# Two gated cross-attention layers with routed experts: four row scatters moved between two subtractions on GpSimd, value and key copies moved to ScalarE, and the row maxima cut in two parts instead of three

## The chip, the core and the metric

The program runs on one core of a Trainium2 chip. It is one launch, and the metric is its time on the device in microseconds (us). The core has five engines with a queue each, which run side by side and meet only at semaphores: PE (TensorE, the matmuls), DVE (VectorE), ACT (ScalarE), POOL (GpSimd) and SP, which here only issues transfers. Each queue is worked off in the order in which it was written.

## The reference

For x of 16 sequences x 256 tokens x 256 numbers, four updates follow one another:

```python
x = x + tanh(g_xattn[0]) * xattn0(layernorm(x), ctx)   # 16 heads of 16, causal mask, biases bv and bo
x = x + tanh(g_ffn[0])   * ffn0(layernorm(x))          # shared expert + top 2 of 8 experts, silu, hidden 256
x = x + tanh(g_xattn[1]) * xattn1(layernorm(x), ctx)   # 16 heads of 16, keys cut at valid_len = 69, no bias
x = x + tanh(g_ffn[1])   * ffn1(layernorm(x))          # top 2 of 8 experts by cosine score, gelu, hidden 1024
```

In `xattn0` the value is `ctx @ Wv.T + bv`, the probabilities of a row sum to one, and the output is `out @ Wo.T + bo`. In `ffn1` the router projects x, divides by the norm of the projection and multiplies with normalised expert vectors.

## The kernel before

Four phases follow one another: the attention phase of layer 0 (`layer_phase`, with the routing of its tokens to experts in it), the expert phase of layer 0 (`expert_phase`), and the same two for layer 1.

**The steps.** An attention phase is a software pipeline over the 16 sequences, in the line `pipeline(engine, step, B, FIRST, LAST, HEAD, TAIL)` of each engine. Step i works on several sequences at once: i.at(3) is turned and split, i.at(2) is projected to q and k, i.at(1) has its scores computed for their row maxima (`score_head`, `row_maxima`), i.at(0) has them computed again, transposed and with the maximum subtracted (`score_head_t`, `exponentials`, `mix_group`), i.at(-1) is projected with Wo and normalised for the router, and i.at(-2) is routed. Steps -3 to 3 are written out, 4 to 9 are a hardware loop over pairs of steps, 10 to 17 are written out again. Within a step every engine goes through the 16 heads, h = 0 to 15, and at a fixed head it does one other job. The order of the work is thus written out by hand, by the `if h == ...` lines of the four `step` functions.

**q and k.** They are split in three bf16 parts. ACT copies q out of PSUM (`evac_q`), DVE copies k (`evac_k`; in layer 1 it multiplies by a mask of valid keys as well). ACT rounds both (`cut_hi`, L1128), POOL subtracts (L693, the first subtraction), ACT rounds the rest (`cut_mid`, L1132, after head 5), POOL subtracts again (L699, the second subtraction). SP then stacks the parts with 24 or 26 transfers.

**Row maxima.** DVE reduces each head's scores (L839 in layer 1), and after heads 7 and 15 `split_max` cuts the negated maxima of 8 heads in three bf16 parts with four small instructions. PE transposes the parts, ACT copies them and issues three small transfers into three rows of the q stack (`stack_max`, L1139 and L1142).

**Value and output.** PE projects v at head 6, DVE copies it into the padded tile, adding bv in layer 0 (`evac_v`, L823 and L825). PE projects the heads with Wo at head 4.

**The router.** PE computes scores for sequence i.at(-2) at head 1 (`gate_rows_of`, L1360) and ACT copies them. In layer 1 ACT also sums the squares of the projection, DVE floors the sum (`floor_ss`, head 2), POOL takes the power -1/2 (`invert_norm`, L669), and DVE scales the scores (`scale_scores`, L888, head 3) before it picks the two best. This chain runs from PE over ACT, DVE and POOL back to DVE. At head 13 PE transposes the normalised rows of i.at(-1) (`turn_route`), ACT copies them at head 14 (`evac_route`, L1199), and the next step's first projection needs their PSUM bank free.

**The scatters.** `send_rows` sends the 2 x 2 tiles of 128 routed rows of i.at(-2) to their experts' regions in DRAM, with four indirect transfers from POOL (L685). They stand last in POOL's step.

Of the kernel before, what the change touches and what calls it, by code (L numbers as in the profile page):

```python
# [5 lines left out]
P = 128  # L6
# [5 lines left out]
ALU = mybir.AluOpType  # L12
# [36 lines left out]
def pipeline(eng, step, count, first, last, head, tail, while_below=None):  # L49
# [8 lines left out]
    with eng.Fori(lo // 2, hi // 2) as pair:  # L58
        with eng.If(pair * 2 < while_below) if while_below is not None else nullcontext():
            step(Step(pair, 0, count))  # L60
            step(Step(pair, 1, count))
# [156 lines left out]
def layer_phase(nc, keep, routed, layer, x_in, ctx_in, lens, weights, biases, F, up_b, gate, shared, load_experts, xs, x_acc):  # L218
# [10 lines left out]
    HH = H // 2  # L229
    VW = 2 * HD  # L230
# [17 lines left out]
    with ExitStack() as ctx:  # L248
# [43 lines left out]
        max_rest = sb("max_rest", [P, TC, H])  # L292
        max_parts = sb("max_parts", [P, TC, 2, 3, HH], BF16)
        max_t = [pair(f"max_t{half}_", [3 * HH, S], BF16) for half in range(2)]
# [6 lines left out]
        if causal:  # L301
            mask_st = sb("mask_st", [P, 2, P], BF16)
            mask_ts = sb("mask_ts", [P, 2, P], BF16)
            bv_rows = sb("bv_rows", [P, TC, D])
# [98 lines left out]
        wo_spread = sem("wo_spread")  # L403
        x_loaded = sems("x_loaded")
# [28 lines left out]
        max_r1 = sem("max_r1")  # L433
        max_mid = sem("max_mid")
# [61 lines left out]
        N_CONSTS = 3 if causal else 1  # L496
# [4 lines left out]

        FIRST, LAST, HEAD, TAIL = -3, B + 1, 7, 8
# [15 lines left out]
        def _(sp):  # L518
# [5 lines left out]
            if causal:  # L524
                bv, bo = biases
                for c in range(TC):
                    sp.dma_start(bv_rows[:, c], bv.rearrange("(a d) -> a d", a=1).to_broadcast((P, D))).then_inc(consts_loaded, 16)
# [16 lines left out]
            sp.wait_ge(consts_ready, N_READY)  # L544

# [42 lines left out]
        def _(pool):  # L588
# [125 lines left out]
        def _(dve):  # L714
# [43 lines left out]
            ln_stats(0, 0, 0)  # L758
            dve.wait_ge(stats_done, 1)
            ln_mean(0)  # L760
            ln_apply(0, 0)

            dve.wait_ge(r_consts_ready, 1)
            dve.wait_ge(r_loaded, 16 * N_LOADS)
# [1137 lines left out]
```

## Time and profile before

| | us |
|---|---|
| median of 3 runs | 1856.92 |
| lowest, highest of the runs | 1847.23, 1857.61 |
| the profiled execution's own time | 1850.12 |
| its span, first to last instruction | 1848.4 |
| attention phase of layer 0 | about 0 to 567 |
| expert phase of layer 0 | about 567 to 830 |
| attention phase of layer 1 | about 830 to 1380 |
| expert phase of layer 1 | about 1380 to 1848 |

Over the whole span PE is busy 82%, DVE 63%, POOL 39% and ACT 38%, at a mean granted TensorE clock of 0.936. These are averages over four phases that have different limits, so they are to be read by stage. "Idle before" in a row is the time for which an engine stood still ahead of an instruction, and behind it stands the engine that ended the wait.

### The profile page before, as it was taken

How to read it: one execution, taken by the hardware profiler on the slowest of the kernel's cores; microseconds unless marked ns; L12 is line 12 of the kernel's file. 1: busy time of each engine (PE TensorE's matmuls, PEld its weight loads, DVE VectorE, ACT ScalarE, POOL GpSimd, SP SyncE). 2: the span in 40 equal slices, each digit the busy share in tenths (PEclk: the TensorE clock that was granted, in tenths of full speed). 3: DMA queues.
4: the chain of work that ended last, by engine and by line, in shares of the span. 5: the costliest groups of instructions: out<-in, count | busy, mean ns of one | idle time of the engine just before them, and what ended most of it. 6: DMA issues, size and time to landing. Idle time of an engine off the chain costs nothing. (4 is left out here: it accounts for less than half of the span.)

```text
span 1848.4 us, 44757 instructions
## 1 busy us (share of the span) xinstructions
PE 1509.7 (82%) x14491; PEld 1253.5 (68%) x14492; DVE 1165.4 (63%) x3254; ACT 707.4 (38%) x1516; POOL 724.4 (39%) x616
## 2 busy tenths in 40 slices
PE   3799988999982777844888888888752999999997
PEld 2677877788761566633566666666432999999996
DVE  4678876878762334334778888887752455555543
ACT  2344534444430111102354544554421444444443
POOL 4234333344233655553123333333235344446422
PEclk9899999999996999975799999999985999999998
DMA  2433333232214666651323332332225233333322
GB/s 89 106 83 102 95 86 97 81 105 79 80 36 137 115 120 112 115 104 54 99 78 109 92 111 81 110 83 82 71 69 177 59 69 91 91 89 85 87 46 40
DMA packets 211174, 167.03 MB, mean 90 GB/s; under 512 B 23042, under 2 KB 203620, under 8 KB 210788
## 3 DMA queue, kind: packets, MB, share of 16 engines
q1 hardware_dynamic: 179556, 124.56, 24.4%
q0 software_dynamic: 28416, 40.03, 11.7%
q8 instruction: 71, 1.16, 0.3%
q10 hardware_dynamic: 3072, 0.79, 0.2%
q14 instruction: 59, 0.48, 0.1%
HBM read 63.40 MB, written 50.51 MB: 62 GB/s over the span
## 5 line engine op out<-in xcount | busy, mean ns | idle before, releaser
L839 DVE TENSOR_REDUCE a_row_max<-a_scores 128x2 f32<-128x512 f32 x256 | 172.3, 683 | 53.3 <-PE a_scores L1455 49.7
L1693 POOL DMA_INDIRECT out_rows<-e_y,e_token x68 | 110.5, 1625 | 239.2 <-DVE e_y L1749 219.3
L1163 ACT ACTIVATE a_probs<-a_scores_t 128x384 f32<-128x384 f32 (+1 forms) x256 | 132.2, 546 | 163.6 <-PE a_scores_t L1470 82.1
L1163 ACT ACTIVATE a_w_rows<-a_scores_t 128x384 f32<-128x384 f32 (+1 forms) x256 | 138.7, 543 | 142.6 <-PE a_scores_t L1473 74.2
L1775 ACT ACTIVATE e_h<-e_h,t_up_bias 128x256 f32<-128x256 f32 x272 | 110.3, 444 | 206.2 <-PE e_h L1811 206.2
L685 POOL DMA_INDIRECT routed_rows_dram<-r_rows,r_slot x128 | 125.6, 981 | 96.4 <-issue 96.4
L1826 PE MATMUL e_y_bank<-e_down_hi,e_hidden_hi 128*128 128x256 f32 x544 | 157.9, 290 | 0.4 <-DVE e_hidden_lo L1722 0.3
L1811 PE MATMUL e_h<-e_xs_hi,e_up_hi 128*128 128x256 f32 x544 | 155.4, 286 | 1.8 <-DVE e_xs_lo L1714 1.6
L1811 PE MATMUL e_h<-e_xs_lo,e_up_hi 128*128 128x256 f32 x544 | 154.7, 284 | 0.0
L1811 PE MATMUL e_h<-e_xs_hi,e_up_lo 128*128 128x256 f32 x544 | 154.6, 284 | 0.0
L1826 PE MATMUL e_y_bank<-e_down_lo,e_hidden_hi 128*128 128x256 f32 x544 | 153.8, 283 | 0.0
L1826 PE MATMUL e_y_bank<-e_down_hi,e_hidden_lo 128*128 128x256 f32 x544 | 153.8, 283 | 0.0
L1693 POOL DMA_INDIRECT x_mid_dram<-e_y,e_token x76 | 118.5, 1560 | 87.4 <-DVE e_y L1749 45.2
L1744 DVE TENSOR_TENSOR e_y_biased<-e_y_bank,t_down_bias 128x512 f32<-128x512 f32 x72 | 49.8, 691 | 131.2 <-PE e_y_bank L1826 131.2
L798 DVE RECIPROCAL a_den_recip<-a_pv 128x128 f32<-128x128 f32 x128 | 116.9, 936 | 23.3 <-PE a_pv L1494 16.5
L693 POOL TENSOR_TENSOR a_rest<-a_qk,a_parts 128x1024 f32<-128x1024 f32 x32 | 67.9, 2123 | 155.7 <-ACT a_parts L1128 155.7
L1789 PE MATMUL e_turned<-ident,e_xs_rows 128*128 128x128 f32 x296 | 46.9, 282 | 98.6 <-DMA e_xs_rows<-routed_rows_dram 98.4
L1455 PE MATMUL a_scores<-a_k_stack,a_q_stack 98*128 98x256 bf16 x512 | 102.2, 283 | 25.1 <-DVE a_row_max L839 16.5
L1722 DVE TENSOR_TENSOR e_hidden_lo<-e_h,e_hidden_hi 128x512 fp32r<-128x512 f32 x136 | 91.3, 687 | 49.5 <-ACT e_hidden_hi L1764 49.2
L836 DVE TENSOR_REDUCE a_row_max<-a_scores 128x1 f32<-128x128 f32 x256 | 72.6, 284 | 76.1 <-PE a_scores L1452 75.5
L699 POOL TENSOR_TENSOR a_parts<-a_rest,a_parts 128x1024 bf16<-128x1024 f32 x32 | 68.5, 2142 | 116.4 <-ACT a_parts L1132 116.4
L1789 PEld LDWEIGHTS e_turned<-ident,e_xs_rows 128*128 128x128 f32 x296 | 34.1, 143 | 111.3 <-DMA e_xs_rows<-routed_rows_dram 109.9
(267 smaller groups left out, 4673.5 us busy)
## 6 DMA issues: line engine op xcount, KB each, us to landing
a_q_stack<-a_parts SPq DMA_DIRECT2D x384, 64.0 KB, 2.7
a_k_stack<-a_parts SPq DMA_DIRECT2D x384, 64.0 KB, 2.6
e_xs_rows<-routed_rows_dram SPq DMA_DIRECT2D x76, 258.0 KB, 3.2
a_ctx_rows<-in_ctx SPq DMA_DIRECT2D x32, 256.0 KB, 3.1
t_up<-in_L_ffn_W SPq DMA_DIRECT2D x8, 1024.0 KB, 5.0
t_down<-in_L_ffn_W SPq DMA_DIRECT2D x8, 1024.0 KB, 7.6
x_rows<-in_x SPq DMA_DIRECT2D x16, 256.0 KB, 3.1
x_mid_dram<-x_rows SPq DMA_DIRECT2D x16, 256.0 KB, 2.9
```

Of the source, the lines that this page charges most:

```text
L685: pool.indirect_dma_start(out=xs, out_offset=bass.IndirectOffsetOnAxis(ap=slot[p][:, k, c:c + 1], axis=0), in_=rows[p][:, k, c, :], in_off ...
L798: nc.vector.reciprocal(den_recip[:, m, cols], pv[m][:, S + part * P:S + part * P + P]).then_inc(recip_done, 1)
L836: nc.vector.reduce_max(row_max[:, 0, h:h + 1], bank[:, 0:P], AX_X)
L839: nc.vector.reduce_max(row_max[:, :, h], bank[:].rearrange("p (c t) -> p c t", c=TC), AX_X).then_inc(maxed, 1)
L1163: nc.scalar.activation(probs[h % NP][:, 0:width], scores_t[h % 2][:, 0:width], ACT.Exp).then_inc(probs_ready, 1)
L1455: last = nc.tensor.matmul(bank[:, c * S:(c + 1) * S], q[at, h, c * P:(c + 1) * P], k[at, h, :], start=True, stop=True)
L1693: pool.indirect_dma_start(out=x_acc, out_offset=bass.IndirectOffsetOnAxis(ap=token[p][:, c:c + 1], axis=0), in_=y[p][:, c, :], in_offset=N ...
L1722: nc.vector.tensor_tensor(lo, h_bank[g][:], hi.bitcast(F32), ALU.subtract).then_inc(hidden_cut, 1)
L1775: nc.scalar.activation(out, h_bank[g][:, at:at + TS], act_func, bias=routed.up_bias[:, bass.ds(e * FC + fc, 1)]).then_inc(hidden_ready, 1)
L1789: last = nc.tensor.transpose(turned[:, kc * TS + c * P:kc * TS + c * P + P], xs_rows[n][:, c, kc * P:(kc + 1) * P], keep.ident[:])
L1811: last = nc.tensor.matmul(h_bank[g][:, at:at + TS], w[:, kc, fc * P:(fc + 1) * P], x[:, kc, :], start=(kc == 0 and term == 0), stop=(kc == ...
L1826: last = nc.tensor.matmul(y_bank[:, c * D:(c + 1) * D], x[:, fc, c * P:(c + 1) * P], w[:, fc, :], start=(fc == 0 and term == 0), stop=(fc ...
```

## The change

It has six parts, in both attention phases unless a layer is named.

1. `send_rows` works on sequence i.at(-3) instead of i.at(-2), a step later, and stands between POOL's two subtractions, ahead of `invert_norm`. The waits on its rows stand ahead of the first subtraction. POOL's pipeline has one step more at the end.
2. `evac_v` is on ACT, after the exponential behind the head of the v projection. In layer 0 `evac_k` is on ACT too, before the first exponential of the step; in layer 1 it stays on DVE.
3. The bias bv no longer goes into v. Once at the start of layer 0, PE multiplies it with Wo, and DVE adds the product to bo.
4. The negated row maxima have two bf16 parts (`MP = 2`) with two DVE instructions for 8 heads, and `stack_max` issues one transfer instead of three.
5. `copy_rows` on ACT works on i.at(-2) at head 10, instead of i.at(-1) at head 13.
6. In layer 1 the router's scores move from head 1 to 2, the Wo projection from 4 to 5, the v projection from 6 to 8, the ranking from 9 to 10 and the transpose of the context (`turn_ctx`) from 12 to 13, each with what follows it on the other engines. In layer 0 these places are as before, but for `mark_chosen`, which goes from head 6 to 5. On DVE `split_max(i, 1)` stands ahead of `add_shared`.

```diff
+        GATE_AT, O_AT, V_AT, RANK_AT, CTX_AT = (1, 4, 6, 9, 12) if soft else (2, 5, 8, 10, 13)
@@ POOL
+            def rows_are_whole(i):
+                pool.wait_ge(rows_ready, i.at(-3) + 1)
+                pool.wait_ge(rows_copied, i.at(-3) + 1)
             def send_rows(i):
-                b, p = i.at(-2), i.par(-2)
-                wait_apart(pool, rows_ready, b + 1, consts_ready, 1)
-                pool.wait_ge(rows_copied, b + 1)
+                b, p = i.at(-3), i.par(-3)
+                if not i.has(2):
+                    rows_are_whole(i)
                 for k in range(2):
                     for c in range(TC):
                         pool.indirect_dma_start(...)
             def step(i):
                 if i.has(2):
+                    if i.has(-3):
+                        rows_are_whole(i)
                     pool.wait_ge(part_hi, b + 1)
                     nc.gpsimd.tensor_tensor(rest[:], qk[:], parts[p][:, :, 0, :], ALU.subtract).then_inc(part_rest, 1)
+                if i.has(-3):
+                    send_rows(i)
                 if not soft and i.has(-2):
                     invert_norm(i)
...
-                if i.has(-2):
-                    send_rows(i)
-            pipeline(pool, step, B, FIRST, LAST, HEAD, TAIL)
+            pipeline(pool, step, B, FIRST, LAST + 1, HEAD, TAIL + 1)
@@ DVE
-                nc.vector.scalar_tensor_tensor(out=max_rest[:, :, hs], ...).then_inc(max_r1, 1)
-                dve.wait_ge(max_r1, n)
-                nc.vector.tensor_copy(max_parts[:, :, half, 1, :], max_rest[:, :, hs]).then_inc(max_mid, 1)
-                dve.wait_ge(max_mid, n)
-                nc.vector.tensor_tensor(max_parts[:, :, half, 2, :], max_rest[:, :, hs], max_parts[:, :, half, 1, :],
-                                        ALU.subtract).then_inc(max_ready, 1)
+                nc.vector.scalar_tensor_tensor(out=max_parts[:, :, half, 1, :], in0=row_max[:, :, hs], scalar=-1.0,
+                                               in1=max_parts[:, :, half, 0, :], op0=ALU.mult, op1=ALU.subtract).then_inc(max_ready, 1)
+            if causal:
+                dve.wait_ge(bv_mixed, 1)
+                nc.vector.tensor_tensor(bo_rows[:], bo_rows[:], stage[1][:, D:2 * D], ALU.add).then_inc(bo_summed, 1)
...
-                if i.has(2):
+                if not causal and i.has(2):
                     evac_k(i)
@@ ACT
-                for j in range(3):
-                    act.dma_start(q_stack[p][MAX_ROW + j:MAX_ROW + j + 1, half * HH:half * HH + HH, :],
-                                  turned[j * HH:(j + 1) * HH, :]).then_inc(max_stacked[half][p], 16)
+                act.dma_start(q_stack[p][MAX_ROW:MAX_ROW + MP, half * HH:half * HH + HH, :], turned[:]).then_inc(max_stacked[half][p], 16)
+                if causal and i.has(2):
+                    evac_k(i)
                 for h in range(H):
                     if i.has(0):
                         exponentials(i, h)
+                    if h == V_AT + 1 and i.has(1):
+                        evac_v(i)
...
-                    if h == 12 and i.has(3):
+                    if h == CTX_AT and i.has(3):
                         evac_ctx(i)
                     if h == 13 and i.has(1):
                         stack_max(i, 1, 0)
-                    if h == 13 and i.has(-1):
+                    if h == 10 and i.has(-2):
                         copy_rows(i)
```

The queue of POOL in the loop of layer 1, before (one step; a_rest is the first subtraction, r_proj_rnorm is `invert_norm`, a_parts the second subtraction, the DMA row the four scatters):

```order
L693 TENSOR_TENSOR a_rest<-a_qk,a_parts 128x1024
L669 TENSOR_TENSOR r_proj_rnorm<-r_proj_ss_min,a_minus_half 128x2
L699 TENSOR_TENSOR a_parts<-a_rest,a_parts 128x4x256
L661 REGISTER_ALU
L662 TENSOR_TENSOR r_var_eps<-r_mean_var,a_eps 128x2
L664 TENSOR_TENSOR r_rstd<-r_var_eps,a_minus_half 128x2
L618 REGISTER_ALU
L619 TENSOR_TENSOR a_var_eps<-a_mean_var,a_eps 128x2
L621 TENSOR_TENSOR a_rstd<-a_var_eps,a_minus_half 128x2
L685 DMA routed_rows_dram<-r_rows,r_slot 35584x258 x4
```

and the same step of the change:

```order
L706 TENSOR_TENSOR a_rest<-a_qk,a_parts 128x1024
L696 DMA routed_rows_dram<-r_rows,r_slot 35584x258 x4
L676 TENSOR_TENSOR r_proj_rnorm<-r_proj_ss_min,a_minus_half 128x2
L714 TENSOR_TENSOR a_parts<-a_rest,a_parts 128x4x256
L668 REGISTER_ALU
L669 TENSOR_TENSOR r_var_eps<-r_mean_var,a_eps 128x2
L671 TENSOR_TENSOR r_rstd<-r_var_eps,a_minus_half 128x2
L625 REGISTER_ALU
L626 TENSOR_TENSOR a_var_eps<-a_mean_var,a_eps 128x2
L628 TENSOR_TENSOR a_rstd<-a_var_eps,a_minus_half 128x2
```

The four scatters have gone from behind the last small operation to a place directly behind the first subtraction and directly ahead of r_proj_rnorm.

The queue of PE near the end of a step of layer 1, heads 12 to 15, before (a_ctx_rows is `turn_ctx`, a_max_parts the transpose of the maxima, r_rows is `turn_route`, the two a_pv rows a `mix_group`):

```order
L1293 MATMUL a_stage<-ident,a_ctx_rows 128x128 x4
L1321 MATMUL a_stage<-ident,a_max_parts 24x128 x2
L1455 MATMUL a_scores<-a_k_stack,a_q_stack 128x256 x2
L1473 MATMUL a_scores_t<-a_q_stack,a_k_stack 128x256 x2
L1494 MATMUL a_pv<-a_probs,a_v_pad 32x256 x8
L1494 MATMUL a_pv<-a_probs,a_ones_pad 32x256 x8
L1293 MATMUL a_stage<-ident,r_rows 128x128 x4
L1455 MATMUL a_scores<-a_k_stack,a_q_stack 128x256 x2
```

and of the change:

```order
L1349 MATMUL a_stage<-ident,a_max_parts 16x128 x2
L1483 MATMUL a_scores<-a_k_stack,a_q_stack 128x256 x2
L1501 MATMUL a_scores_t<-a_q_stack,a_k_stack 128x256 x2
L1522 MATMUL a_pv<-a_probs,a_v_pad 32x256 x8
L1522 MATMUL a_pv<-a_probs,a_ones_pad 32x256 x8
L1321 MATMUL a_stage<-ident,a_ctx_rows 128x128 x4
L1321 MATMUL a_stage<-ident,r_rows 128x128 x4
L1483 MATMUL a_scores<-a_k_stack,a_q_stack 128x256 x2
```

`turn_ctx` now stands directly ahead of `turn_route`, which waits for ACT's copy of the maxima; on ACT that copy stands behind the copy of what `turn_ctx` writes, as before.

## Rows read from the trace of the kernel before

**Rows 1.** The page, part 5 (costliest groups): busy us, mean ns | idle before
```profile
L839 DVE TENSOR_REDUCE a_row_max<-a_scores 128x2 f32<-128x512 f32 x256 | 172.3, 683 | 53.3 <-PE a_scores L1455 49.7
```

**Rows 2.** Busy time by stage: us, then each engine's busy time (instructions), clock, DMA
```profile
96.00:560.00 464.00, 426.11 (x5508) 356.39 (x5508) 363.65 (x1253) 206.18 (x455) 176.77 (x167) 0.98 0.31 85
...
905.00:1375.00 470.00, 398.32 (x4042) 275.30 (x4035) 380.76 (x1054) 227.95 (x488) 151.45 (x159) 0.99 0.32 89
...
1425.00:1848.40 423.40, 409.02 (x3397) 407.67 (x3396) 215.96 (x387) 192.34 (x409) 174.99 (x82) 0.98 0.34 72
```

**Rows 3.** Timeline of POOL, layer 1: start us, us, instruction [idle before <-releaser]
```profile
1075.16 2.12 POOL L693 TENSOR_TENSOR a_rest<-a_qk,a_parts 128x1024 f32<-128x1024 f32 x1 [4.84 <-ACT a_parts L1128]
1077.39 0.71 POOL L669 TENSOR_TENSOR r_proj_rnorm<-r_proj_ss_min,a_minus_half 128x2 f32<-128x2 f32 x1
1081.94 2.14 POOL L699 TENSOR_TENSOR a_parts<-a_rest,a_parts 128x1024 bf16<-128x1024 f32 x1 [3.83 <-ACT a_parts L1132]
...
1095.34 1.04 POOL L685 DMA_INDIRECT routed_rows_dram<-r_rows,r_slot  x1 [1.33 <-issue]
...
1099.22 0.96 POOL L685 DMA_INDIRECT routed_rows_dram<-r_rows,r_slot  x1 [0.30 <-issue]
1105.10 2.12 POOL L693 TENSOR_TENSOR a_rest<-a_qk,a_parts 128x1024 f32<-128x1024 f32 x1 [4.92 <-ACT a_parts L1128]
```

**Rows 4.** Timeline of DVE, the same step of layer 1
```profile
1076.20 0.69 DVE L839 TENSOR_REDUCE a_row_max<-a_scores 128x2 f32<-128x512 f32 x1 [1.23 <-PE a_scores L1455]
...
1078.22 0.48 DVE L888 TENSOR_SCALAR r_gate_scores<-r_raw_scores,r_proj_rnorm,r_temp_recip 128x8 f32<-128x8 f32 x2 [0.32 <-POOL r_proj_rnorm L669]
...
1082.51 0.69 DVE L839 TENSOR_REDUCE a_row_max<-a_scores 128x2 f32<-128x512 f32 x1 [0.99 <-PE a_scores L1455]
...
1085.50 0.68 DVE L825 COPY a_v_pad<-a_stage 128x512 f32<-128x512 f32 x1
...
1087.03 0.18 DVE L850 SCALAR_TENSOR_TENSOR a_max_rest<-a_row_max,a_max_parts 128x16 f32<-128x16 f32 x1
...
1100.21 1.77 DVE L798 RECIPROCAL a_den_recip<-a_pv 128x128 f32<-128x128 f32 x2 [0.69 <-PE a_pv L1494]
...
1103.19 0.69 DVE L791 TENSOR_TENSOR a_qk<-a_stage,a_valid 128x512 f32<-128x512 f32 x1
```

**Rows 5.** Timeline of PE, the same step of layer 1
```profile
1091.76 1.07 PE L1494 MATMUL a_pv<-a_probs,a_v_pad 128*32 128x256 f32 x16
...
1093.63 0.66 PE L1293 MATMUL a_stage<-ident,r_rows 128*128 128x128 f32 x4
...
1096.61 0.47 PE L1303 MATMUL a_stage<-a_xn_t,a_w_hi 128*128 128x256 f32 x2 [1.45 <-ACT r_xn_t L1199]
...
1104.02 2.02 PE L1360 MATMUL a_stage<-r_gate_w,r_xn_t 128*128 128x264 f32 x8 [1.26 <-DVE a_qk L791]
```

**Rows 6.** Timeline of ACT, the same step of layer 1
```profile
1090.71 0.59 ACT L1155 ACTIVATE a_ctx_t<-a_stage 128x512 fp32r<-128x512 f32 x1
...
1092.36 0.36 ACT L1139 ACTIVATE a_max_t<-a_stage 24x256 bf16<-24x256 bf16 x1
1092.75 1.97 ACTq L1142 DMA_DIRECT2D a_q_stack<-a_max_t  x3
```

**Rows 7.** Timeline of POOL, layer 0, two steps' first subtractions
```profile
186.08 2.12 POOL L693 TENSOR_TENSOR a_rest<-a_qk,a_parts 128x1024 f32<-128x1024 f32 x1 [1.98 <-ACT a_parts L1128]
...
215.94 2.12 POOL L693 TENSOR_TENSOR a_rest<-a_qk,a_parts 128x1024 f32<-128x1024 f32 x1 [1.65 <-ACT a_parts L1128]
```

**Rows 8.** Timeline of PE, layer 0: start, one steady step, the loop's entry
```profile
28.13 1.08 PE L1293 MATMUL a_stage<-ident,a_xn 128*128 128x128 f32 x4 [6.03 <-DVE r_sh_down_bias L767]
...
201.83 0.23 PE L1448 MATMUL a_scores<-a_mask_st,ident 128*128 128x128 bf16 x1 [0.70 <-DVE a_row_max L837]
...
211.16 0.28 PE L1321 MATMUL a_stage<-ident,a_max_parts 128*24 128x128 bf16 x2 [0.76 <-DVE a_max_parts L855]
...
248.92 0.23 PE L1448 MATMUL a_scores<-a_mask_st,ident 128*128 128x128 bf16 x1 [3.81 <-DVE a_row_max L837]
```

More of the change, by code:

```diff
@@ L57, in pipeline @@
     assert lo % 2 == 0 and (hi - lo) % 2 == 0
[L58 to L61, printed above, removed]
+    if lo < hi:
+        with eng.Fori(lo // 2, hi // 2) as pair:
+            with eng.If(pair * 2 < while_below) if while_below is not None else nullcontext():
+                step(Step(pair, 0, count))
+                step(Step(pair, 1, count))
     for i in range(hi, last + 1):
@@ L291, in layer_phase @@
         row_max = sb("row_max", [P, TC, H])
-        max_rest = sb("max_rest", [P, TC, H])
-        max_parts = sb("max_parts", [P, TC, 2, 3, HH], BF16)
-        max_t = [pair(f"max_t{half}_", [3 * HH, S], BF16) for half in range(2)]
+        max_parts = sb("max_parts", [P, TC, 2, MP, HH], BF16)
+        max_t = [pair(f"max_t{half}_", [MP * HH, S], BF16) for half in range(2)]
         probs = [sb(f"probs{n}", [P, 512]) for n in range(NP - 4)] + [w_rows[:, n].rearrange("p c d -> p (c d)") for n in range(4)]
@@ L723, in _ @@
             if causal:
-                nc.vector.tensor_scalar(bo_rows[:], bo_rows[:], keep.tanh_gates[:, gate_col:gate_col + 1], None, ALU.mult).then_inc(bo_gated, 1)
+                for m in range(KC):
+                    src = ctx_rows[1][:, 0, m * P:(m + 1) * P].rearrange("p (half n d) -> p half n d", half=2, d=HD)
+                    for half in range(2):
+                        last = nc.vector.tensor_copy(bv_rows[:, m, :, half, :], src[:, half])
+                last.then_inc(bv_spread, 1)
             else:
@@ L777, in evac_k @@
                 need(dve, part_rest, b)
-                if causal:
-                    dve.wait_ge(k_done, b + 1)
-                    nc.vector.tensor_copy(qk[:, KC:2 * KC, :].rearrange("p c s -> p (c s)"), stage[0][:]).then_inc(k_ready, 1)
-                else:
+                if not causal:
                     n = bass.ds(b, 1)
@@ L992, in step @@
                         row_maxima(i, h)
-                    if h == 2 and not soft and i.has(-2):
+                    if h == GATE_AT + 1 and not soft and i.has(-2):
                         floor_ss(i)
-                    if h == 3 and i.has(-2):
+                    if h == GATE_AT + 2 and i.has(-2):
                         if not soft:
@@ L1222, in step @@
                         cut_mid(i)
-                    if h == 6 and i.has(-2):
+                    if h == GATE_AT + 5 and i.has(-2):
                         route_exps(i)
@@ L1257, in _ @@
             pe.wait_ge(consts_ready, N_READY)
+            if causal:
+                pe.wait_ge(bv_spread, 1)
+                for m in range(KC):
+                    last = nc.tensor.transpose(stage[0][:, m * P:(m + 1) * P], bv_rows[:, m].rearrange("p n half d -> p (n half d)"), keep.ident[:])
+                last.then_inc(bv_turned, 1)
+                pe.wait_ge(bv_copied, 1)
             pe.wait_ge(r_loaded, 16 * N_LOADS)
@@ L1267, in _ @@
                 pe.wait_ge(prep_copied, 3)
+                for m in range(KC):
+                    last = nc.tensor.matmul(stage[1][:, D:2 * D], bv_cols[:, m, :], wo_t[:, m, :], start=(m == 0), stop=(m == KC - 1))
+                last.then_inc(bv_mixed, 1)
+                pe.wait_ge(bo_gated, 1)
             else:
@@ L1514, in step @@
                             mix_group(i, 0, h // GH - 1)
-                    if h == 1 and i.has(-2):
+                    if h == GATE_AT and i.has(-2):
                         gate_rows_of(i)
```

93 lines of the change are left out of this document (50 added, 43 removed).

## The prediction, made before the change was run

> **What bounds the kernel now.** The busy times by stage come first [rows 2]. From 96 to 560 us, the steady part of layer 0's attention phase, PE is busy 426 of 464 us (92%) and DVE 364: PE is nearly the bound. From 905 to 1375 us, layer 1's attention phase, PE is busy 398 of 470 us (85%) and DVE 381 (81%): neither is full, so the step is set by how the two wait for each other. From 1425 us on PE is busy 409 of 423 us in layer 1's experts; the change does not touch that stage, nor layer 0's experts. Then the timelines of one steady step. First subtractions are 29.94 us apart in layer 1 [rows 3] and 29.86 us in layer 0 [rows 7]. In the step of layer 1 DVE's larger waits are 1.23, 0.32, 0.99 and 0.69 us [rows 4], so some 26.7 of its 29.9 us are filled, small gaps counted as filled. PE's larger ones are 1.45 us for ACT's copy of the router's columns and 1.26 us for DVE's copy of k [rows 5]. The reader should see that layer 1 has hardly three us of slack per step on DVE, and that every wait put into DVE's queue there comes out of it.
>
> **1. The scatters behind the first subtraction, layer 1.** This is the largest term. Before, the power -1/2 starts 0.11 us after the first subtraction ends (1077.28 to 1077.39), and DVE waits only 0.32 us for it before it scales the scores [rows 3, 4]. After, four scatters stand between the two. Four take 4.84 us from the start of the first to the end of the last (1095.34 to 1100.18) [rows 3]; with 0.17 us ahead of the first, about 5.0 us. The chain counted from the end of DVE's copy of k (1103.19 + 0.69 = 1103.88) [rows 4] is: first subtraction starts 1.22 us later (1105.10) and ends at +3.3, scatters end at +8.4, power at +9.2 us. DVE's own way there: three maxima at 0.6 us from start to start (0.68 us mean, overlapping a little) [rows 1], then a wait for head 3. PE can begin head 2 only after the first maximum (+0.7), and computes the two scores of head 2 (0.45), the router's scores (about 1.9 of the 2.02 in [rows 5]) and head 3, whose scores reach DVE at about +3.6, so this wait is 1.7 us. Two more maxima and the floor bring DVE to +5.0. It then waits until +9.2: **4.2 us**. DVE's waits in this stretch go from 1.23 + 0.32 + 0.99 = 2.54 us to 1.7 + 4.2 = 5.9: +3.4 us per step. PE cannot fill this: two heads after the stalled maximum it needs that score bank again. The added wait is on DVE's in-order queue, and behind it stand the maxima of all further heads, for which PE waits. Second subtraction: it starts after the power, at +9.3 us, against +1.2 + 6.8 = +8.0 now (it starts 6.78 us after the first) [rows 3]; 1.3 us later, and SP's stacking, which the next step needs, stays covered, since half a step lies between.
>
> **2. Work taken off DVE.** The value copy, 0.68 us with 0.6 from start to start; two small instructions in each of the two `split_max`, 0.18 us each with 0.2 from start to start [rows 4]. Together 0.6 + 4 x 0.2 = 1.4 us per step in layer 1. It counts there, as DVE is what stalls: -1.4.
>
> **3. The moved heads at the end of layer 1's step.** `turn_ctx` now stands ahead of `turn_route`, and `turn_route` waits for ACT's copy of the maxima, which stands behind ACT's copy of the context: 0.2 + 0.5 + 0.4 + 0.1 = 1.2 us in which PE stands still, by the 0.59 and 0.36 us copies and their latencies [rows 6]. Before, `turn_route` follows the probabilities' matmuls without a wait [rows 5]. Against it, the transfers on ACT fall from three in 1.97 us to one, between 0.66 us (a third) and 1.97 us; I take 0.7, as each moves one or two short rows. With `copy_rows` gone from there, the 1.45 us wait for ACT shrinks to about 0.9. DVE's idle time ahead of the maximum of head 14 becomes about 2.0 us, for the 0.69 us that falls away: +1.3 per step. Between +0 (all in DVE's backlog) and +2.0.
>
> Layer 1's step: +3.4 - 1.4 + 1.3 = **+3.3 us**. Both subtraction and scatters are in steps 3 to 13, 11 steps: +36 us. Three more full steps (2, 14, 15) have the moved heads and the relief but no scatters in between. Of the step's 3.3 us, 2.0 are the scatters': the moved heads alone already make DVE and PE wait there, so removing the scatters would not give back all of the 3.4. The three get +1.3 each, +4.
>
> **4. Layer 0.** There is no power -1/2 here. The scatters take 5.0 us of the pause that POOL has between the subtractions, and end at about the time of the second one (0.8 us late, covered by SP's slack). At the other end they free nothing: the first subtraction waits 1.65 us for ACT, not for POOL [rows 7]. So they count zero; if the cover fails, 0.8 us per step. PE's two waits in a steady step are 0.70 and 0.76 us [rows 8]. The 0.76 goes to about 0.4: `turn_max_late` gets its maxima two instructions (0.4) earlier, and then waits for `add_shared`, which is now behind them. The 0.70 stays, since it follows a dense stretch of DVE in heads 10 and 11 that the change leaves alone; smaller PE waits of 0.2 to 0.3 near it go. Sum -0.65 us per step, between -0.4 and -1.5 (both gone): 14 steps, **-9 us**. k's and v's copies on ACT cost 0.6 us each (by the 0.59 us copy of the same size) and are hidden: ACT is busy 206 of 464 us [rows 2]. At the loop's entry DVE comes late and PE waits 3.81 us [rows 8], once more at a later pair; without the k copy in DVE's queue 0.6 us less each: -1.
>
> **5. The start.** bv's product with Wo and the sum delay POOL's first addition, and with it all constants that follow on POOL and PE's first transpose at 28.13 [rows 8], by two DVE instructions and part of an ACT copy: +1 us, between 0 and 3.
>
> **Sum.** +36 + 4 - 9 - 1 + 1 = +31 us on the profiled execution's 1850.1, so 1881. That execution is 6.8 us below the median of three runs; 1857 + 31 = 1888. I predict **1885 us**.
>
> **Rivals.** (a) *The scatters hardly hold POOL* (0.10). No row shows a POOL computation directly behind a scatter in layer 1, and spans on POOL are rough. If POOL is free soon after the first subtraction, the power comes in time: layer 1's steps are +1.3 x 14 = +18, with -9 for layer 0: 1850 + 9 to 1857 + 9, about 1863. Against it stands the even pace: from the first scatter to the fourth 3.88 us, 1.3 us each [rows 3]. The Trainium skill ("DMA: Bandwidth & Descriptors", Anatomy of one DMA — SWDGE (gpsimd) path) says that generating descriptors is a small part and that many can be emitted before the cost shows; by that rule this rival would be the likeliest, with its 1863, but the trace's 4.84 us for four speaks against it.
>
> (b) *The relief wins, faster* (0.09). One mechanism: DVE's wait ahead of the scaling stays below 0.32 + 1.4 = 1.7 us, because PE's other work between fills it, and the shorter DVE queue carries both layers. Then layer 1 gains about 1.1 us in 14 steps (-15), layer 0 both PE waits, 1.46 us in 14 steps (-20): 1857 - 34 = 1823. For it: 1.4 us less on an engine that is nearly full. Against it: the 4.2 us are an in-order chain from k's copy to the power, and nothing in the change shortens it.
>
> (c) *Half of the stall is absorbed* (0.07): PE's waits of 1.45 and 1.26 us and the new ones overlap, +1.5 x 11 - 9 + 5 = +13: 1867.
>
> (d) *The second subtraction's delay reaches the next step* (0.06): the stacked q and k come late for its first head, layer 1 at +5 us in 14 steps: 1857 + 61 = 1918. SP's half step of slack speaks against it.
>
> (e) *The move of the scatters does nothing in layer 0* is part of the forecast, not apart from it.
>
> **Numbers.** The forecast has 0.68, with a range of its own of 1868 to 1905, from 2.3 to 4.3 us per step in layer 1 and -4 to -20 in layer 0. Less than 1% (18.6 us), about what a measurement of this kernel can tell from no change, are (a) and (c): 0.17. Slower are the forecast and (d): 0.74. Faster is (b): 0.09. The range leaves out (b), most of (d) and little else: 1858 to 1908.
>
> **What would show it.** In layer 1's steps 3 to 13: a row of DVE at the scaling of the scores with some 4 us ahead of it, released by POOL's power; the four scatters directly ahead of that power; steps of about 33 us between first subtractions; PE waiting 1 us or more at the maxima of heads 5 to 7 and 1.2 us at `turn_route`. In layer 0: steps of 29.2 us, the wait at L1321 down to 0.4. Wrong would be the forecast if DVE waits under 1.7 us at the scaling, if layer 1's steps are below 31 us, or if the second subtraction of layer 0 now waits behind the scatters and delays the stacking.

## The result, and the profile after

| | before | after |
|---|---|---|
| time, median (lowest to highest), us | 1857.14 (1847.23 to 1857.61), 4 runs | 1903.46 (1892.39 to 1906.62), 4 runs |
| profiled execution, us (its span) | 1850.12 (1848.4) | 1906.62 (1904.9) |
| step of layer 1, mean of 10, us | 30.0 | 35.8 |
| step of layer 0, steady, us | 29.9, with four of 32 to 34 | 29.2 to 29.5, all |

The ratio is 1.0262, 95% interval [1.0232, 1.0291]: 2.6% slower, +46 us of medians. The two profiled executions are 56.5 us apart, since the one of after was the slowest of its four. That difference, read at the first subtractions: start +3.5, layer 0's attention phase -22.9, between the phases +2.5, layer 1's attention phase +69.2, the rest +4.1.

Busy time by stage, columns as in [rows 2], then the costliest group of the page (answers to [rows 1]):

```profile
96.00:560.00 464.00, 422.94 (x5538) 356.91 (x5528) 338.26 (x1217) 217.31 (x486) 181.43 (x172) 0.96 0.33 93
905.00:1375.00 470.00, 379.95 (x3484) 258.28 (x3485) 327.30 (x843) 207.15 (x431) 132.87 (x135) 0.92 0.28 79
1481.00:1904.90 423.90, 409.69 (x3396) 408.43 (x3395) 215.84 (x387) 192.65 (x409) 175.10 (x82) 0.98 0.34 72
```
```profile
L847 DVE TENSOR_REDUCE a_row_max<-a_scores 128x2 f32<-128x512 f32 x256 | 171.5, 684 | 105.0 <-PE a_scores L1483 102.8
```

The experts' stage is unchanged (423.9 against 423.4 us). In layer 1's attention phase all engines are less busy than before, and the granted clock of TensorE is 0.92 instead of 0.99. DVE's idle time ahead of its maxima doubled, from 53 to 105 us.

POOL in one step of layer 1 (answers to [rows 3]), then DVE in the same step ([rows 4]):

```profile
1085.37 2.12 POOL L706 TENSOR_TENSOR a_rest<-a_qk,a_parts 128x1024 f32<-128x1024 f32 x1 [11.70 <-ACT a_parts L1144]
...
1091.54 0.96 POOL L696 DMA_INDIRECT routed_rows_dram<-r_rows,r_slot  x1 [0.30 <-issue]
1092.53 0.73 POOL L676 TENSOR_TENSOR r_proj_rnorm<-r_proj_ss_min,a_minus_half 128x2 f32<-128x2 f32 x1
1093.22 2.12 POOL L714 TENSOR_TENSOR a_parts<-a_rest,a_parts 128x1024 bf16<-128x1024 f32 x1
```
```profile
1083.30 0.69 DVE L810 TENSOR_TENSOR a_qk<-a_stage,a_valid 128x512 f32<-128x512 f32 x1
1083.91 1.88 DVE L847 TENSOR_REDUCE a_row_max<-a_scores 128x2 f32<-128x512 f32 x3
1088.65 0.69 DVE L847 TENSOR_REDUCE a_row_max<-a_scores 128x2 f32<-128x512 f32 x1 [2.87 <-PE a_scores L1483]
...
1093.37 2.21 DVE L891 TENSOR_SCALAR r_gate_scores<-r_raw_scores,r_proj_rnorm,r_temp_recip 128x8 f32<-128x8 f32 x2 [3.26 <-POOL r_proj_rnorm L676]
...
1098.11 0.18 DVE L915 TENSOR_TENSOR r_one_hot<-r_expert_iota,r_top_index_f 128x32 f32<-128x32 f32 x1
```

Three things are to be seen. The scatters hold POOL: the power starts as the fourth ends (1091.54 + 0.96), and DVE waits 3.26 us for it where it waited 0.32. **The scaling itself takes 2.21 us instead of 0.48**: it runs beside the second subtraction (1093.22 to 1095.34), which before started only 3.2 us after the scaling had ended. And DVE waits 2.87 us for the fourth head's scores; before it was 1.23 us, for the third head's.

PE in the same step and at the matching place of the next (answers to [rows 5]):

```profile
1084.65 0.39 PE L1483 MATMUL a_scores<-a_k_stack,a_q_stack 98*128 98x256 bf16 x2 [1.93 <-DVE a_row_max L847]
1085.10 3.09 PE L1388 MATMUL a_stage<-r_gate_w,r_xn_t 128*128 128x264 f32 x8
...
1096.57 0.39 PE L1483 MATMUL a_scores<-a_k_stack,a_q_stack 98*128 98x256 bf16 x2 [2.13 <-DVE a_row_max L847]
...
1109.18 0.66 PE L1321 MATMUL a_stage<-ident,r_rows 128*128 128x128 f32 x4 [0.94 <-ACT a_max_t L1155]
...
1111.54 0.47 PE L1331 MATMUL a_stage<-a_xn_t,a_w_hi 128*128 128x256 f32 x2 [0.83 <-ACT r_xn_t L1213]
...
1131.21 0.61 PE L1483 MATMUL a_scores<-a_k_stack,a_q_stack 98*128 98x256 bf16 x2 [3.19 <-DVE a_row_max L847]
```

The router's scores took 3.09 us here, 2.02 in [rows 5], and the pair of scores after the 3.19 us wait 0.61 us, elsewhere 0.39. The busy table in stretches of 6 us shows why; the column after POOL is the granted clock:

```profile
1120.00:1126.00 6.00, 5.72 (x55) 3.56 (x54) 2.04 (x4) 4.09 (x11) 5.09 (x4) 1.00 0.57 177
1126.00:1132.00 6.00, 2.81 (x16) 1.87 (x14) 3.88 (x11) 0.60 (x1) 3.78 (x3) 0.84 0.12 44
1132.00:1138.00 6.00, 6.00 (x42) 4.83 (x44) 4.23 (x15) 2.52 (x6) 0.89 (x2) 0.59 0.30 77
1138.00:1144.00 6.00, 5.50 (x79) 2.94 (x71) 4.58 (x17) 3.15 (x6) 0.00 (x0) 1.00 0.22 56
```

After the stall PE runs for some 6 us at the lower level (1.2 GHz; 0.59 is mostly that) and is full meanwhile (6.00 of 6.00): the wait is paid a second time in slow matmuls. Two steps of before and two of after, from one first subtraction to the next:

```profile
1105.10:1135.24 30.14, 26.16 (x268) 18.48 (x267) 25.99 (x71) 15.21 (x32) 10.68 (x11) 1.00 0.36 100
1135.24:1165.16 29.92, 25.90 (x266) 18.18 (x265) 26.03 (x71) 15.21 (x32) 10.67 (x11) 1.00 0.34 95
```
```profile
1085.37:1120.02 34.65, 28.13 (x266) 18.99 (x265) 25.11 (x67) 15.72 (x33) 10.65 (x12) 0.95 0.29 82
1120.02:1156.94 36.92, 29.33 (x268) 20.14 (x267) 25.43 (x67) 15.97 (x34) 10.65 (x12) 0.91 0.29 81
```

The same matmuls (266 to 268) keep PE busy 2.2 to 3.2 us longer. In layer 0 (answers to [rows 7] and [rows 8]) the scatters fill POOL's pause as forecast, and steps are 29.5 us:

```profile
185.25 2.13 POOL L706 TENSOR_TENSOR a_rest<-a_qk,a_parts 128x1024 f32<-128x1024 f32 x1 [6.49 <-ACT a_parts L1144]
...
191.43 0.96 POOL L696 DMA_INDIRECT routed_rows_dram<-r_rows,r_slot  x1 [0.31 <-issue]
192.41 2.15 POOL L714 TENSOR_TENSOR a_parts<-a_rest,a_parts 128x1024 bf16<-128x1024 f32 x1
214.77 2.13 POOL L706 TENSOR_TENSOR a_rest<-a_qk,a_parts 128x1024 f32<-128x1024 f32 x1 [6.31 <-ACT a_parts L1144]
```
```profile
200.99 0.23 PE L1476 MATMUL a_scores<-a_mask_st,ident 128*128 128x128 bf16 x1 [0.70 <-DVE a_row_max L845]
210.06 0.27 PE L1349 MATMUL a_stage<-ident,a_max_parts 128*16 128x128 bf16 x2 [0.51 <-issue]
```

### The profile page after: what moved, and what is told of

It is laid out like the page before. It is cut to its first block and busy times, and to the rows that moved or that the text cites. A ratio compares the mean times of both kernels' runs of the same rounds, so it can differ in the third digit from the quotient of the medians.

```text
span 1904.9 us, 44507 instructions
## 1 busy us (share of the span) xinstructions
PE 1547.1 (81%) x14497; PEld 1275.4 (67%) x14498; DVE 1113.4 (58%) x3083; ACT 730.8 (38%) x1565; POOL 725.1 (38%) x616
## 5 line engine op out<-in xcount | busy, mean ns | idle before, releaser
L1177 ACT ACTIVATE a_probs<-a_scores_t 128x384 f32<-128x384 f32 (+1 forms) x256 | 137.0, 546 | 113.8 <-PE a_scores_t L1501 58.4
L1483 PE MATMUL a_scores<-a_k_stack,a_q_stack 98*128 98x256 bf16 x512 | 107.0, 294 | 75.3 <-DVE a_row_max L847 66.4
L1483 PEld LDWEIGHTS a_scores<-a_k_stack,a_q_stack 98*128 98x128 bf16 x512 | 40.5, 102 | 119.1 <-DVE a_row_max L847 90.8
```

The costliest lines, as they stand in the source:

```text
L1177: nc.scalar.activation(probs[h % NP][:, 0:width], scores_t[h % 2][:, 0:width], ACT.Exp).then_inc(probs_ready, 1)
L1483: last = nc.tensor.matmul(bank[:, c * S:(c + 1) * S], q[at, h, c * P:(c + 1) * P], k[at, h, :], start=True, stop=True)
```

## The experiments

Three groups, each on one chip, with the kernel before beside them. It took 1851.87 us in the first group, 1941.89 in the second, on another chip, and 1851.80 in the third. So times of the second group are compared only within it; first and third are compared by their ratios to the kernel before. "Step" is the mean of ten steps of layer 1, the fifth first subtraction to the fifteenth. All ratios carry 95% intervals.

### First group: is it the scatters or the heads?

**The power ahead of the scatters.** Edit:
```diff
-                if i.has(-3):
-                    send_rows(i)
                 if not soft and i.has(-2):
                     invert_norm(i)
+                if i.has(-3):
+                    send_rows(i)
```


> The changed kernel with one edit: in layer 1's step the power -1/2 of the norm stands ahead of the four scatters, which stay between the two subtractions. Theory A (the scatters ahead of the power hold VectorE at the scaling of the scores): the wait of 3 to 4.5 us there falls below 0.8 us, layer 1's steps go from 36.1 us to 31 to 32.5 us, and the time falls by 40 to 55 us to 1850 to 1863 us. Theory B (the moved heads of layer 1 and the new order at the end of its step carry the loss): the steps stay above 34 us and the time above 1885 us. In between, 1865 to 1885 us, would mean that both carry a part, or that scatters between the subtractions cost in some other way, for instance because the second subtraction now ends later than its readers can bear.

Measured: 1899.81 us, ratio 1.0282 [1.0243, 1.0322]; step 35.2 us. DVE's wait at the scaling fell to 0.29 us as theory A said, yet nothing came back. DVE, POOL and PE of one step:

```profile
1150.49 2.52 DVE L910 CAST r_top_index_f<-r_top_index 128x4 f32<-128x4 uint32 x1
1152.92 0.74 DVE L832 SCALAR_TENSOR_TENSOR x_rows<-a_stage,tanh_gates,x_rows 128x512 f32 x1
```
```profile
1150.84 2.13 POOL L714 TENSOR_TENSOR a_parts<-a_rest,a_parts 128x1024 bf16<-128x1024 f32 x1
```
```profile
1153.81 0.48 PE L1340 MATMUL a_stage<-a_w_hi,a_ctx_t 128*128 128x256 f32 x2 [2.56 <-DVE x_rows L832]
```

The scatters still put off the second subtraction, and that now meets the cast of the indices (128x4): 2.52 us instead of 0.16, ended 0.04 us after the subtraction. The x update waits behind it on DVE, and PE 2.56 us for the x update. The wait had only changed its place. The time lies in theory B's band, but the cause is the third one named there, the scatters between the subtractions. (The cast's row starts 0.35 us ahead of the subtraction's; in all 11 steps with scatters it takes 2.44 to 2.60 us and ends 0.03 to 0.04 us after the subtraction.)

**The scatters back at the step's end**, the rest of the change kept:
```diff
-                if i.has(-3):
-                    send_rows(i)
...
                     rstd_of(i.at(4))
+                if i.has(-2):
+                    send_rows(i)
```


> The changed kernel with the four scatters back at the end of POOL's step, where they were before, so that all the rest of the change stands alone. Theory A: layer 1's steps are 31 to 31.5 us (29.94 of the kernel before, plus the 1.3 us that the prediction gave to the moved heads), layer 0's stay at 29.2 to 29.5, and the time is 1845 to 1860 us. Theory B: layer 1's steps stay above 34 us, 1885 us or more. If layer 0's steps rise, the scatters' new place was what helped layer 0, against the prediction, which counted it as zero there.

Measured: 1853.41 us, ratio 1.0005 [0.9981, 1.0028]. Taking the scatters' place back gives back the whole loss of the result. Layer 0's steps are 29.3 us here too, so the new place gives nothing there on this chip. But layer 1's step is 32.6 us, not 31.2: something in the rest costs more than the prediction gave it. Two of its steps, and two stretches of the first of them:

```profile
968.00:972.00 4.00, 4.00 (x15) 2.84 (x13) 0.90 (x2) 1.22 (x5) 2.12 (x1) 0.57 0.61 185
...
968.33:1002.54 34.21, 29.74 (x268) 20.41 (x267) 25.34 (x67) 15.76 (x34) 10.65 (x12) 0.90 0.31 85
...
992.00:996.00 4.00, 3.74 (x24) 3.03 (x28) 3.75 (x9) 1.29 (x3) 2.14 (x3) 0.57 0.52 150
...
1069.18:1100.17 30.99, 26.45 (x266) 18.06 (x265) 23.61 (x67) 15.60 (x33) 10.68 (x11) 1.00 0.32 92
```
```profile
967.76 0.39 PE L1480 MATMUL a_scores<-a_k_stack,a_q_stack 98*128 98x256 bf16 x2 [1.84 <-DVE a_row_max L844]
968.22 3.37 PE L1385 MATMUL a_stage<-r_gate_w,r_xn_t 128*128 128x264 f32 x8
```

At full clock the step is 31.0 us, as forecast. In the other step the clock fell twice: at the router's scores, after a wait of 1.84 us ahead of them (0.57 from 968 to 972 us), and 24 us later, behind the waits at the step's end (0.57 from 992 to 996 us). Over the eleven steps from 934 us on, three without such a fall take 31.0 to 31.7 us, five with one 32.0 to 32.8, and three with two 33.9 to 34.2. Each fall goes with 1 to 1.5 us more.

**Only the scatters moved**, on the kernel before:
```diff
+                if i.has(-3):
+                    send_rows(i)
                 if not soft and i.has(-2):
                     invert_norm(i)
...
                     rstd_of(i.at(4))
-                if i.has(-2):
-                    send_rows(i)
```

> The kernel before with only the four scatters moved to a step later, between the two subtractions and ahead of the power. Theory A: VectorE waits 3 to 4.5 us at the scaling, and the second subtraction runs beside the scaling and stretches it; layer 1's steps are 34 to 36 us, and the time is 1900 to 1925 us, as layer 0's gain is missing too. By the prediction's own price of the scatters alone (3.4 us in 11 steps) it would be 1894 us. Theory B: 1850 to 1865 us, as without the moved heads the wait is filled.

Measured: 1935.51 us, ratio 1.0459 [1.0432, 1.0485]; step 36.7 us, settling at 37.5. Worse than theory A's upper end. DVE and PE:

```profile
1186.31 2.20 DVE L895 TENSOR_SCALAR r_gate_scores<-r_raw_scores,r_proj_rnorm,r_temp_recip 128x8 f32<-128x8 f32 x2 [5.26 <-POOL r_proj_rnorm L670]
```
```profile
1189.51 0.61 PE L1462 MATMUL a_scores<-a_k_stack,a_q_stack 98*128 98x256 bf16 x2 [4.20 <-DVE a_row_max L846]
```

5.26 us of wait, 1.7 of stretched scaling, PE still for 4.20 us and then partly at the lower clock in every step (mean 0.91). Layer 0's steady steps are 30.6 us here against 29.9 before: without the relief of DVE the scatters' new place costs 0.7 us per step there too.

**Layer 1's heads at their old places**, the scatters where the change has them:
```diff
-        GATE_AT, O_AT, V_AT, RANK_AT, CTX_AT = (1, 4, 6, 9, 12) if soft else (2, 5, 8, 10, 13)
+        GATE_AT, O_AT, V_AT, RANK_AT, CTX_AT = (1, 4, 6, 9, 12)
```


> The changed kernel with layer 1's router scores, output projection, value projection, rank and context turn back at heads 1, 4, 6, 9 and 12 instead of 2, 5, 8, 10 and 13. Theory A: the wait for the power grows by what the earlier scaling adds (about one head, 1.5 us), but the wait at the turned router rows goes; the time stays within 12 us of the changed kernel's 1903 us. Theory B: the time falls by more than 20 us, below 1883 us.

Measured: 1887.29 us, ratio 1.0197 [1.0175, 1.0219]; step 36.1 us. Against the kernel before, this is 9 to 12 us below the changed kernel (1.0244 and 1.0262), where theory A allowed 12 us and theory B wanted more than 20. Steady steps are no shorter; what is saved is in the early ones without scatters (28.9 us where the change has 34.2).

### Second group

**Scatters at the end and old places**: both edits above; what is left is the relief of DVE.

> The changed kernel with two parts taken back: the scatters stand at the end of POOL's step again, and layer 1's heads are at their old places (1, 4, 6, 9, 12). What is left is the relief of VectorE (k's and v's copies of layer 0 and v's of layer 1 on ScalarE, two-part maxima, one transfer). Theory D (the moved heads cost layer 1 the 2.6 us per step by which the version with the scatters at the end is above the kernel before): layer 1's steps fall from 32.6 to between 28.8 and 30 us, layer 0's stay at 29.3, and the time is 1810 to 1830 us. Rival E (what costs layer 1 there is the copies on ScalarE and the order at the step's end, not the places): layer 1's steps stay at 32 us or more and the time within 8 us of 1853.

Measured: 1913.38 us beside 1941.89, ratio 0.9862 [0.9834, 0.9889]; step 31.7 us. The bands were for a chip like the first, so they decide nothing; the version was repeated in the third group. On this chip layer 0's steps are 35 us. DVE and ACT at the turn of one of them, and how often (from the list of waits, 130 to 440 us):

```profile
295.74 1.77 DVE L814 RECIPROCAL a_den_recip<-a_pv 128x128 f32<-128x128 f32 x2 [4.76 <-remote]
```
```profile
DVE a_den_recip L814 <- remote: 41.9, 9, 4.9
```
```profile
ACT a_max_t L1152 <- remote: 53.1, 9, 6.0
```

The columns of the last two are us in total, times, longest. Nothing in the trace releases these waits; both engines stand at once, at the turn of the step, while the step's scatters are in flight (DMA share 0.61 to 0.76 from 290 to 299 us).

**Two scatters and two**:
```diff
                 if i.has(-3):
-                    send_rows(i)
+                    send_rows(i, -3, (1,))
...
                     rstd_of(i.at(4))
+                if i.has(-2):
+                    rows_are_whole(i)
+                    send_rows(i, -2, (0,))
```

> The changed kernel with two of the four scatters back at the end of POOL's step and two left between the first subtraction and the power. If the loss goes by the length of the wait alone, half of it comes back: VectorE waits about 0.7 to 2 us at the scaling instead of 3.3 to 4.5, and the time is 1872 to 1884 us, half way between 1903 and 1853. If the loss lies in what a long stall sets off (TensorE's lower granted clock after it, the second subtraction beside the scaling), more than half comes back: 1853 to 1868 us. If two scatters hold as four do: above 1890 us.

Measured: 1899.87 us, ratio 0.9796 [0.9758, 0.9834]. The bands were for a chip like the first, so they decide nothing. By the trace, DVE waits 8.2 us in nine steps for the power (1.9 us in three of them, 0.3 to 0.5 in six), the two scalings take 2.3 to 2.4 us in four steps and 0.48 in the others, layer 1's step is 33.3 us, and layer 0's steps are 30.1 us where the version above has 35.

**A quarter of the second subtraction** in layer 1:
```diff
-                    nc.gpsimd.tensor_tensor(parts[p][:, :, 2, :], rest[:], parts[p][:, :, 1, :], ALU.subtract).then_inc(parts_ready, 1)
+                    n = slice(0, 1) if not soft and i.has(-2) else slice(0, 2 * KC)
+                    nc.gpsimd.tensor_tensor(parts[p][:, n, 2, :], rest[:, n], parts[p][:, n, 1, :], ALU.subtract).then_inc(parts_ready, 1)
```


> The changed kernel with POOL's second subtraction of layer 1 cut to a quarter of its columns in the steps that have scatters; the low parts of the other columns are left out. Theory F (a small VectorE instruction that starts while the subtraction runs ends only with it): the two scalings take 0.5 to 0.8 us instead of 2.2, and layer 1's steps fall by 1.5 to 2.5 us, the time to 1872 to 1890 us. If the length of the scaling only covered a wait that was there anyway, the scalings are short, but the steps stay within 0.5 us and the time within 8 us of 1903.

Measured: 1914.62 us, ratio 0.9864 [0.9841, 0.9887]. Without the changed kernel on this chip its time says nothing of the cut; it was repeated in the third group. Its layer 0 is that of the changed kernel, with all four scatters between the subtractions: the steps there are 29.2 to 31.3 us, and DVE has no stall at their turn, where the version with the scatters at the end has 35 us.

**Layer 0's copy of k on ACT**, alone, on the kernel before:
```diff
-                if causal:
-                    dve.wait_ge(k_done, b + 1)
-                    nc.vector.tensor_copy(qk[:, KC:2 * KC, :].rearrange("p c s -> p (c s)"), stage[0][:]).then_inc(k_ready, 1)
...
+                act.wait_ge(k_done, b + 1)
+                nc.scalar.activation(qk[:, KC:2 * KC, :].rearrange("p c s -> p (c s)"), stage[0][:], ACT.Copy).then_inc(k_ready, 1)
```


> The kernel before with one edit: layer 0's copy of k stands on ScalarE instead of VectorE. Layer 0's steady steps are 29.9 us in the kernel before, with three of 33 to 34 where VectorE stands 3.3 and 1.2 us at the loop's turn with nothing to wait for. If 0.6 us less in VectorE's queue is what makes that stall vanish: all of layer 0's steps at 29.3 to 30 us and the time 12 to 20 us below the kernel before. If the stall stays and only the queue is shorter: 0 to 8 us below. Layer 1 is the same program and should not move.

Measured: 1935.04 us, ratio 0.9968 [0.9955, 0.9982], 7 us less. The stalls at the step's turn stay (DVE 35.0 us in eight), so the question of the first chip's loop entry was not answered.

### Third group: one chip, like the first

**The changed kernel again.**

> The changed kernel itself once more, beside the three others and the kernel before on one chip, because the chip of the second group of runs gave the kernel before 1942 us where the first gave it 1852. Theory G (on a chip like the second, engines stand 3 to 6 us at layer 0's step turns while the scatters of the step's end run, and the change takes them from there): where the kernel before takes about 1940 us, this one takes 1905 to 1925 us, a gain; where the kernel before takes about 1855 us, this one takes 1895 to 1907 us, the loss seen first. Without such an effect of the place in layer 0 it is 2.3 to 2.9% slower on any chip.

Measured: 1897.81 us, ratio 1.0244 [1.0219, 1.0269], step 35.8 us: the result again. Whether the change gains on a chip like the second was not run. An estimate: the quarter version took 1914.62 us there, and in this group the changed kernel takes 1897.81 to its 1876.48; with the same proportion it would take some 1936 us beside 1942, no clear gain.

**Scatters at the end and old places, again.**

> Scatters at the end of POOL's step in both layers, layer 1's heads at their old places, the relief of VectorE kept; it was 1.4% faster than the kernel before on the second chip, with layer 0's steps at 35 us and layer 1's at 31.7. On a chip where the kernel before takes about 1855 us: layer 0's steps 29.3 us, layer 1's 28.8 to 30 us, 1810 to 1830 us. On one where it takes 1940 us: again about 1913 us.

Measured: 1802.93 us, ratio 0.9727 [0.9708, 0.9747]. Layer 0's steps 29.3, layer 1's 28.8 us. One step:

```profile
1098.30:1127.01 28.71, 25.70 (x266) 18.21 (x265) 24.23 (x66) 15.46 (x33) 10.67 (x12) 1.00 0.36 102
```

**Layer 0's scatters between the subtractions, layer 1's at the end, old places:**
```diff
-                if i.has(-3):
+                if soft and i.has(-3):
                     send_rows(i)
...
+                if not soft and i.has(-2):
+                    send_rows(i)
```

> As the run with scatters at the end and old places, but layer 0's scatters stay between the two subtractions, as in the changed kernel; only layer 1's stand at the step's end. Each layer has the place that its own rows favour, so this is the version that should beat both kernels. Theory G: on a chip where the kernel before takes 1940 us, layer 0's steps fall from 35 to 30 us and the time is 1850 to 1870 us; on one where it takes 1855 us layer 0's steps are 29.3 us either way and the time is that of the run with both at the end within 6 us. If the place in layer 0 does nothing, it equals that run on any chip.

Measured: 1802.79 us, ratio 0.9725 [0.9707, 0.9743]. It equals the version above on this chip, so no effect of the place in layer 0 shows. That it would be better on the second chip wasn't run. For it speaks that the quarter version, with the same layer 0, needs 422 us there from layer 0's first to its last first subtraction, and the version with the scatters at the end 466: an estimate of 44 us less, 1869 us. Both beat the kernel before by 49 us and the changed kernel by 95.

**A quarter of the second subtraction, beside the changed kernel.**

> The changed kernel with layer 1's second subtraction cut to a quarter of its columns (the low parts of the other columns are left out), now beside the changed kernel on the same chip. In the earlier run the two scalings took 0.75 us instead of 2.2 and layer 1's steps were 34.2 us. Theory F (holding VectorE's small instructions costs the step): 15 to 28 us below the changed kernel of this group. If it only filled a wait: within 8 us of it.

Measured: 1876.48 us, ratio 1.0147 [1.012, 1.0174], against 1.0244 [1.0219, 1.0269]: 21 us less, as theory F said. Step 33.9 us against 35.8.

```profile
1074.79 0.75 DVE L892 TENSOR_SCALAR r_gate_scores<-r_raw_scores,r_proj_rnorm,r_temp_recip 128x8 f32<-128x8 f32 x2 [2.85 <-POOL r_proj_rnorm L676]
```

The wait for the power is still there (2.85 us in this step, 4.5 to 4.7 in most), and the stretch is nearly gone: the two scalings take 0.75 us and end with the shorter subtraction. The cut also ends the subtraction 1.5 us earlier for its readers; that PE doesn't wait for the stacked q and k in the steady steps of the changed kernel speaks against a part of that.

## Why the prediction was right, and where it was short

Direction and mechanism were right: slower, by the wait for the power. The size was not: +46 us of medians against +31 (the point was 1885), and +56.5 against +31 by the profiled executions. That 1903 us still lies in 1858 to 1908 is luck. Layer 1's step grew by 5.8 us, above the forecast's own 2.3 to 4.3, and its phase by 69 us where some 37 were forecast; layer 0's phase shrank by 23 us where 10 were forecast. With layer 0 as forecast, the median would lie near 1916 us, outside the range.

Layer 1's step, from pairs of versions that differ in one part. The two of a pair did not always run on the same chip; the changed kernel's step was 35.8 us on both of its chips.

| term, us per step | forecast | measured | from |
|---|---|---|---|
| relief of DVE | -1.4 | -1.2 | before 30.0; end, old places 28.8 |
| moved heads | +1.3 (0 to 2.0) | +3.8 | end, old places 28.8; end, new places 32.6 |
| scatters, on top of both | +3.4 | +3.2 | end, new places 32.6; changed 35.8 |
| sum | +3.3 | +5.8 | before 30.0; changed 35.8 |
| scatters alone | - | +6.7 | before 30.0; only scatters 36.7 |

**1. The scatters.** "It then waits until +9.2: 4.2 us" was right: 32.0 us in 8 steps between 1000 and 1300 us, 4.0 each. Where the router's scores ran at full clock, DVE waited 1.5 us for head 3 (1.7 forecast), elsewhere 2.8 to 3.2. The prediction prices the scatters twice: +3.4 in its sum, and 2.0 as what would come back without them, since its steps without scatters keep +1.3. Measured with both other parts in place: +3.2, and +2.6 without the scatters. So the +3.4 agrees and the 2.0 doesn't, and the agreement is partly luck. The moved heads had already dropped the clock in eight of eleven steps, and they bring the scaling later, so that the wait is 4.0 us instead of 5.3 with the old places; there the same scatters cost 6.7 to 7.2 us per step. What the step left out are two things: the second subtraction, for which it only looked whether its own readers (SP's stacking) can bear 1.3 us of delay, meets another DVE instruction (+1.7 at the scaling, -0.8 at `r_one_hot`; the quarter subtraction gave 1.9 us per step back), and the lower clock after a stall.

**2. The relief** was right: -1.2 for -1.4 in layer 1.

**3. The moved heads: here the step failed.** The waits that it named came nearly as told (0.94 us at `turn_route` for 1.2, 0.8 at `project_q` for 0.9, one transfer on ACT). What term 3 left at nothing is PE's wait at the step's start and the clock. The router's scores now stand behind the third head's, PE waits 1.5 to 1.9 us for DVE there, and after 1.84 us (and 1.93 in the changed kernel) the eight matmuls ran at the lower clock; where they did, they took 2.9 to 3.6 us instead of 2.0. Behind the waits at the step's end the clock fell as well (992 to 996 us in the version with the scatters at the end). At full clock the version with the scatters at the end is at 31.0 to 31.7 us, +2.2 to +2.9 for the heads, already above the upper end that the forecast gave them, 2.0; with one fall of the clock it is at 32.0 to 32.8, with two at 34. With the heads at their old places and the scatters at the end no steady step shows a clock below 1.00. The five moves were not run one by one, so which of them costs how much is read from the rows only.

**4. Layer 0.** Steps of 29.2 forecast, 29.2 to 29.5 measured. The scatters cost nothing there, as forecast, but only beside the relief; alone they cost 0.7 us per steady step, near the 0.8 that the prediction named if the cover fails. At the loop's entry 1 us was forecast and some 13 came: the steps of 33.8, 32.0, 34.0 and 33.2 us were all 29.3 to 29.5. DVE's stalls of 3.3 and 1.2 us there, for which the trace names no other work, are gone. They stay when only the scatters move (34.1, 32.5, 33.7, 31.9) and are gone with the relief and the scatters at the end, so the relief did it; which part of it is open. The wait of 0.70 us stayed, that of 0.76 at `turn_max_late` became 0.51.

**5. The start** took +2 to +3.5 us, against 1 (0 to 3).

**The rivals.** (a) fell: a power starts where the fourth scatter ends. The Trainium skill ("DMA: Bandwidth & Descriptors", Anatomy of one DMA — SWDGE (gpsimd) path), by which this would have been the likeliest, doesn't hold for a POOL instruction right behind four scatters: their 5.0 us were paid in full. (b) fell for this change; the relief by itself does win, and more than that rival gave it (49 us against 34). (c) fell; nothing was absorbed. (d) fell as told, as PE doesn't wait for the stacks in the steady steps, though near its size (1918): the delay of the second subtraction cost through DVE instead.

## What to carry to other kernels

When a block of POOL is moved, list for every POOL instruction behind it which instructions of DVE it will now run beside, not only who reads its result. Price a stall of TensorE at its length and again for the slow matmuls that may follow, and look at both ends of a step where heads are moved. Parts that share a slack don't add: run them apart; here one part of the change was worth -49 us, and the other two hid it.

## What the runs showed of the hardware

- **Some small DVE instructions that meet a POOL subtraction end with it.** The scaling (128x8) 2.2 us instead of 0.48, a cast (128x4) 2.52 instead of 0.16, before the change `r_one_hot` (128x32) about 1.0 instead of 0.18. Not every one on SBUF is held: the statistics of x (`BATCH_NORM_STATS2`, 128x256, two in 0.74 us) and the index search (128x8, 0.16 us) kept their times beside it, as did the maxima (0.69 us), which read PSUM. The Trainium skill ("GPSIMD Engine Reference", 8. Key points) says that POOL shares its SBUF interfaces with VectorE, with contention for instructions in a two-port mode or with two SBUF inputs. The traces agree for the instructions with two inputs, `r_one_hot` among them; in which mode the scaling and the cast ran, no view shows.
- **The granted clock after a stall.** After 3.19 us of idle PE ran about 6 us at the lower level, after 4.20 us about 7 (1190 to 1197 us, only the scatters moved). After 1.84 and 1.93 us it also fell, after 2.13 us it didn't, and after 1.59 us in the changed kernel it fell once (the router's scores 3.63 us) and otherwise not (1.95), so the length alone doesn't decide.
- **Chips differ.** The kernel before takes 1852 us on two chips and 1942 on a third, where layer 0's steps with scatters at their end are 35 us; there DVE and ACT stand 4 to 6 us at each turn with no releaser in the trace. With two of the four scatters moved the steps are 30.1 us, with all four (the quarter version) 29.2 to 31.3. The stalls and the scatters at the step's end coincide; what the engines stand for stays open.
